# One tanh over the 2304 score columns of a pair of heads

## The chip, the cores and the metric

The kernel runs on one core of a Trainium2 chip. The metric is the device time of one execution in microseconds (us). Five engines work side by side, each through its own list of instructions in order: TensorE (PE, matmuls; PEld is its weight load), VectorE (DVE), ScalarE (ACT), GpSimd (POOL) and SyncE (SP, which issues DMAs). They order their work by semaphores.

## The reference, cut to what matters

The first layer is causal attention with 16 heads of width 8 over 16 batches of 512 rows, with capped scores:

```
scores = jnp.einsum('bhqd,bhkd->bhqk', q, k) / jnp.sqrt(jnp.float32(dk))
scores = jnp.tanh(scores / SOFTCAP) * SOFTCAP
scores = jnp.where(causal[None, None], scores, -jnp.inf)
probs = jax.nn.softmax(scores, axis=-1)
```

It is followed by an output projection, a layer norm, and a second layer that routes 63 rows of each batch through a small attention and an MLP, and another layer norm. `x` is (16, 512, 128) in float32.

## The kernel before, in words

**Groups.** Two heads of a batch are a group; a batch has 8 groups, and the kernel works through 128 of them. The causal scores of a group are kept in transposed blocks: 8 blocks of 64 keys, block kb with 512 - 64 kb query columns, 2304 columns in all, on 128 partitions (64 for each head). They lie in `ps_s`, five PSUM banks; there is only one such buffer. `COL` gives each block's column; the blocks 0, 1 and 7 fill columns 0 to 1023 (two banks), the others columns 1024 to 2303 (three banks).

**The loop.** `iterations` runs `body(p)` for the pairs of batches, each with 16 slots (`for s in range(16)`), and each slot has two halves. Every engine runs the same loop over its own list. PE is one group ahead: in slot s it computes the scores of group s+1 (`scores`, L1186), unit 0 (6 matmuls, 1024 columns) at the start of the first half and unit 1 (10 matmuls, 1280 columns) at the start of the second. Behind each stand the side steps of that half from the table `PE_ORDER`: the preparation of the next batches (`prep.`), probabilities times values (`pv.`, L1202), the end of the first layer (`fin.`), the routing (`route.`), and the second layer of the pairs before (`sel.`, `att.`, `late.`). DVE, POOL and ACT have tables of their own. This order is written out by hand, and each engine keeps to it: a step that waits holds up all behind it.

**ACT.** In slot s ACT computes the tanh of group s in two instructions, one for each unit (L720, `ps_s` to `th`, which has two halves), then a side step if there is one, and then the exp of group s-1 (L735, `th` to the ring `pr`), over all 2304 columns in one instruction. The tanh waits for its unit's scores and for the exp of group s-2.

**Waits of the scores.** A unit of scores waits until the tanh of the same unit of the group before is done (`tanh_done`), as it overwrites what that tanh reads. The other unit can still be read meanwhile.

**Behind the exp.** POOL multiplies the diagonal blocks by a triangle (L631); `pv.0` and `pv.1` need the groups 0 to 3 of a batch, `pv.2` and `pv.3` the groups 4 to 7. SP turns q and k of a later batch by DMA (L549, `turn`) into a buffer whose last reader are the scores of the batch two before.

**Side steps named below.** Of slot 15: `sel.RT` and `prep.xT` (L1225). Slot 0: `sel.msel`, `fin.y0T` | `att.S0`, `prep.qk0`, `att.S1`. Slot 1: `pv.2`, `route.thr` | nothing. Slot 2: `pv.3`, `prep.qk1` | `att.P0`, `prep.v` (L1240). Slot 6: `att.wo` (L1382) | `route.wrow`, `att.h2T` (L1387). Slot 8: `prep.qk0`, `prep.qk1` (L1232) | `fin.y0T` (L1208) and others. Slot 10: `route.won`, `prep.v` (L1240) | `fin.y1T`, `late.w2` (L1400). The bar parts the halves. Slots 4, 7, 9, 11, 12 and 13 have nothing in the first half, so that the two units stand together.

Of the kernel before, what the change touches and what calls it, by code (L numbers as in the profile page):

```python
# [8 lines left out]
ACT = mybir.ActivationFunctionType  # L9
# [7 lines left out]
H, DH = 16, 8  # L17
# [6 lines left out]
SOFTCAP = 50.0  # L24
# [3 lines left out]
QK_SCALE = 64.0  # L28
# [9 lines left out]
NB = S // 64  # L38
COL = {0: 0, 1: 512, 7: 960, 2: 1024, 6: 1408, 3: 1536, 5: 1856, 4: 2048}
GROUP = 2304  # L40
UNIT = ((0, 1024), (1024, GROUP))
UNIT_BLOCKS = ((0, 1, 7), (2, 6, 3, 5, 4))
SIX_FROM = 48
PV_BLOCKS = ((0, 1), (2, 3, 4, 5, 6, 7))

# [1 line left out]
def probs_at(n):  # L47

    return GROUP * (n % 5 if n < SIX_FROM else (5, 3, 4, 0, 1, 2)[(n - SIX_FROM) % 6])


def pv_of(n):

    return 4 * (n // 8) + 2 * (n % 8 // 4) + 2
# [268 lines left out]
def build(nc, x, w_q, w_k, w_v, w_o, amask, pos, router_w, router_b, wq, wk, wv, wo, w1, w2, ln1, ln2, out):  # L323
    ctx = ExitStack()
    with ctx:
        def sb(name, shape, dt=F32):
            return ctx.enter_context(nc.sbuf_tensor(name, shape, dt))

        def sem(name):
            return ctx.enter_context(nc.semaphore(name))  # L330
# [45 lines left out]
        th = sb("th", [P, 2, GROUP])  # L376
# [70 lines left out]
        ps_s = ctx.enter_context(nc.psum_tensor("ps_s", [P, 5 * 512], F32))  # L447
# [17 lines left out]
        scores_ready = sem("scores_ready")  # L465
        tanh_done = sem("tanh_done")
        exp_done = sem("exp_done")
# [22 lines left out]
        def iterations(body):  # L490

            for p in range(-1, PAIRS + 3):
                body(p)

        def run_side(order, table, p, s, half):

            for entry in order[2 * s + half]:
                name, shift = entry.split("@")
                name, _, k = name.partition("/")
                unit = Batch(p + int(shift), int(k)) if k else p + int(shift)  # L500
                if live(unit, B if k else PAIRS):
                    table[name](unit, unit.k if isinstance(unit, Batch) else None)

        def group(p, s, lag=0):

            s -= lag
            b = Batch(p, s // 8)
            return (b, b.k, s % 8) if live(b, B) else None
# [3 lines left out]
        def _(sp):  # L512
# [30 lines left out]
            def turn(b, k):  # L543

                if b.at_least(2):
                    sp.wait_ge(scores_ready, (b - 1).no * 16)
                for s, (dst, part) in enumerate(((q_st, "q"), (k_st, "k"))):
                    pl["prep"].wait(sp, b, f"lo_{part}")
                    sp.dma_start_transpose(out=dst[:, k].rearrange("p g (t n) -> p (g t) n", t=NT),  # L549
                                           in_=st[:, s].rearrange("p g t j c d -> p (g t j c d)")).then_inc(turned[k], 16)  # L550
# [144 lines left out]
        @block.scalar  # L695
        def _(act):
            act.wait_ge(setup_ve, SETUP_RED)
            nc.scalar.activation(turn[:, :, :, :], red[:, :, :, :], ACT.Sin).then_inc(setup_act, 1)

            def att_exp(q, _):  # L700
                ve["att"].wait(act, q, "sub1")
                nc.scalar.activation(pm[:, :, 0:KSEL], pm[:, :, 0:KSEL], ACT.Exp).then_inc(probs_ready, 1)  # L702

            def att_tanh(q, _):
                pl["att"].wait(act, q, "hu")
                nc.scalar.activation(hq[:, :], hu[:, :], ACT.Tanh, scale=float(np.sqrt(2.0 / np.pi)))\  # L706
                    .then_inc(gate_ready, 1)

            table = {"att.exp": att_exp, "att.tanh": att_tanh}

            def body(p):
                for s in range(16):
                    g = group(p, s)
                    if g:
                        b, _, gi = g
                        for u, (c0, c1) in enumerate(UNIT):
                            act.wait_ge(scores_ready, b.no * 16 + (2 * gi + u + 1))
                            if gi >= 2 or b.at_least(1):
                                act.wait_ge(exp_done, b.no * 8 + (gi - 1))
                            nc.scalar.activation(th[:, gi % 2, c0:c1], ps_s[:, c0:c1], ACT.Tanh,  # L720
                                                 scale=1.0 / (QK_SCALE ** 2 * DH ** 0.5 * SOFTCAP))\
                                .then_inc(tanh_done, 1)
                    for half in range(2):
                        run_side(ACT_ORDER, table, p, s, half)
                    g = group(p, s, 1)
                    if g:
                        b, _, gi = g
                        act.wait_ge(tanh_done, b.no * 16 + (2 * gi + 2))

                        n = b.no * 8 + gi  # L730
                        if n >= 5 and n != SIX_FROM:
                            act.wait_ge(pv_done, pv_of(n - (5 if n < SIX_FROM else 6)))
                        if n == SIX_FROM:
                            pe["sel"].wait(act, 1, "R")
                        nc.scalar.activation(pr[:, probs_at(n):probs_at(n) + GROUP], th[:, gi % 2, :], ACT.Exp,  # L735
                                             scale=SOFTCAP).then_inc(exp_done, 1)
            iterations(body)


# [420 lines left out]
        def _(t_):  # L1160
# [15 lines left out]
                tr(ps_y[:, P:P + NPC], pos_f[:, :], ident[0:NPC, 0:NPC])  # L1176
                mm(ps_y[:, 256:257], ones1[:, :], rb_one[:, :], start=True, stop=True).then_inc(setup_pe, 1)

            def scores(b, k, gi, u):

                if gi > 0 or b.at_least(1):
                    t_.wait_ge(tanh_done, b.no * 16 + (2 * gi + u - 1))
                for kb in UNIT_BLOCKS[u]:
                    for s in range(2):
                        rows = slice(32 * (2 * (gi % 2) + s), 32 * (2 * (gi % 2) + s) + 32)
                        last = mm(ps_s[64 * s:64 * s + 64, COL[kb]:COL[kb] + S - 64 * kb],  # L1186
                                  k_st[rows, k, gi // 2, 64 * kb:64 * kb + 64], q_st[rows, k, gi // 2, 64 * kb:S],
                                  start=True, stop=True)
                last.then_inc(scores_ready, 1)
# [234 lines left out]
            def body(p):  # L1424
                for s in range(16):
                    for half in range(2):
                        g = group(p, s, -1)
                        if g and g[2] == 0 and half == 0:
                            t_.wait_ge(turned[g[1]], g[0].pair * 32 + 32)
                        if g:  # L1430
                            scores(g[0], g[1], g[2], half)
                        run_side(PE_ORDER, table, p, s, half)
            iterations(body)


# [26 lines left out]
```

## Time and profile before

| | |
|---|---|
| median of 3 runs | 853.38 us (852.76 to 853.59) |
| profiled execution | 853.79 us, span 851.8 us |
| TensorE clock granted, mean | 0.794 of full speed |
| PE busy | 695.6 us (82%) |
| DVE busy | 588.6 us (69%) |
| ACT busy | 555.5 us (65%) |
| POOL busy | 389.1 us (46%) |

The span runs from the first to the last instruction. Busy is the time in which an engine had an instruction in work; it doesn't say whether anything waited for that work. The view by windows shows the granted clock of a stretch: 1.00 is 2.4 GHz, 0.50 is 1.2 GHz. A row of the timeline gives the start, the duration from first start to last end, the engine, the line, what is written from what is read, the count, and in brackets the idle time before it with what ended it. Ends of matmuls are modelled: the last of a step overlaps the first of the next by some 0.07 us, so that differences of starts are the better measure.

### The profile page before, as it was taken

Reading aid. Unit: us, or ns where it says so; the run is one execution under the profiler, and the core shown is the slowest. Engines: PE = TensorE matmul, PEld = TensorE weight load, DVE = VectorE, ACT = ScalarE, POOL = GpSimd, SP = SyncE. Lnnn points to the kernel's source line nnn. Section 1 sums busy time; section 2 is a strip of 40 time slices with the busy share of each in tenths; the row PEclk is TensorE's granted clock in tenths of the full one; section 3 lists DMA queues with packets and bytes.
Section 4 is the critical chain, followed back from the end, with each engine's and each line's share of the span. In section 5 each row is a group of like instructions: output and inputs, shape, how many; then the busy total and the mean of one; then the engine's idle time right before and its main releaser. Section 6 shows DMA issues by size and latency. Waiting matters only on the chain.

```text
span 851.8 us, 17007 instructions
## 1 busy us (share of the span) xinstructions
PE 695.6 (82%) x6576; PEld 417.3 (49%) x6576; DVE 588.6 (69%) x1681; ACT 555.5 (65%) x403; POOL 389.1 (46%) x399
## 2 busy tenths in 40 slices
PE   3578797998899987898799978998799879874652
PEld 2334344544466454646465545645565545534332
DVE  4442627767768778859676788768785876678355
ACT  0588788879767985877666885868696878600000
POOL 5264435447445663365354654447435644321201
PEclk8567767899769986897697987798798977985755
DMA  6320303033302320030303030220203030000001
GB/s 185 62 52 25 62 13 63 14 65 110 62 14 41 85 53 23 27 75 2 75 27 63 14 63 15 54 47 10 54 27 62 2 62 27 13 1 22 4 0 50
DMA packets 96914, 36.75 MB, mean 43 GB/s; under 512 B 68019, under 2 KB 94147, under 8 KB 96835
## 3 DMA queue, kind: packets, MB, share of 16 engines
q1 hardware_dynamic: 96834, 35.67, 18.4%
q8 instruction: 53, 0.87, 0.4%
q14 instruction: 27, 0.21, 0.1%
HBM read 14.69 MB, written 4.19 MB: 22 GB/s over the span
## 4 chain that ended last, share of the span: by engine, by line
PE 59%; DVE 19%; issue 10%; ACT 8%; POOL 2%; DMA 1%; POOLq 0%; DVEq 0%; ACTq 0%
PE ps_y L1202 16%; PE ps_s L1186 14%; ACT pr L735 4%; ACT th L720 3%; PE ps_a L1232 2%; PE ps_m L1208 2%; PE ps_m L1232 2%; PE ps_m L1356 2%; DVE v_aug L848 2%; PE ps_m L1310 2%; PE ps_m L1260 2%; PE ps_a L1370 2%; PE ps_a L1208 2%; PE ps_a L1393 1%; PE ps_a L1260 1%
## 5 line engine op out<-in xcount | busy, mean ns | idle before, releaser
L720 ACT ACTIVATE th<-ps_s 128x1024 f32<-128x1024 f32 (+1 forms) x256 | 281.1, 1129 | 125.3 <-PE ps_s L1186 116.1
L735 ACT ACTIVATE pr<-th 128x2304 f32<-128x2304 f32 x128 | 271.4, 2121 | 22.2 <-PE ps_y L1202 22.2
L631 POOL TENSOR_TENSOR pr<-pr,tri 128x320 f32<-128x320 f32 (+1 forms) x256 | 193.6, 781 | 182.4 <-ACT pr L735 182.4
L1186 PE MATMUL ps_s<-q_st,k_st 32*64 32x448 f16 (+7 forms) x2048 | 197.7, 332 | 24.8 <-ACT th L720 21.2
L1202 PE MATMUL ps_y<-pr,v_aug 128*32 128x512 f32 (+7 forms) x2048 | 157.2, 451 | 0.4 <-POOL pr L631 0.4
L1186 PEld LDWEIGHTS ps_s<-q_st,k_st 32*64 32x64 f16 x2048 | 95.5, 119 | 116.4 <-issue 44.0
L1202 PEld LDWEIGHTS ps_y<-pr,v_aug 128*32 128x32 f32 x2048 | 61.6, 116 | 76.5 <-issue 58.2
L645 POOL TENSOR_TENSOR st<-qk,st 128x1024 f16<-128x1024 f32 x32 | 73.8, 2326 | 38.9 <-DVE st L864 38.9
L633 POOL TENSOR_TENSOR k_wide<-qkT,head_of 128x1024 f32<-128x1024 f32 x16 | 30.1, 1903 | 65.4 <-DVE qkT L1033 65.4
L633 POOL TENSOR_TENSOR r<-x,rw_row 128x512 f32<-128x512 f32 x16 | 18.9, 1182 | 77.2 <-DVE x L926 77.2
L706 ACT ACTIVATE hq<-hu 128x512 f32<-128x512 f32 x8 | 5.0, 630 | 59.6 <-POOL hu L633 59.6
L874 DVE COPY y_u<-ps_y 128x512 f32<-128x512 f32 x32 | 21.6, 676 | 30.6 <-PE ps_y L1202 30.6
L633 POOL TENSOR_TENSOR st<-qk 128x1024 f32<-128x1024 f32 x16 | 30.9, 1929 | 21.8 <-DVE qk L837 21.7
L950 DVE SCALAR_TENSOR_TENSOR wins<-w_wide,x,later 128x512 f16<-128x512 f32 (+1 forms) x64 | 38.9, 608 | 1.9
L702 ACT ACTIVATE pm<-pm 128x1008 f32<-128x1008 f32 x8 | 8.3, 1037 | 42.7 <-DVE pm L1047 42.7
L633 POOL TENSOR_TENSOR z_base<-x,coef 128x512 f32<-128x512 f32 x16 | 17.1, 1070 | 39.5 <-DVE coef L974 39.5
L1310 PE MATMUL ps_m<-mask_a,E 128*64 128x512 f32 x112 | 29.8, 610 | 0.0
L848 DVE COPY v_aug<-ps_m 64x512 f32<-64x512 f32 x32 | 22.0, 689 | 9.8 <-PE ps_m L1240 9.3
L1232 PE MATMUL ps_m<-wT,xT 128*128 128x256 f32 x64 | 26.5, 556 | 0.9 <-DVE xT L832 0.9
L1387 PE MATMUL ps_m<-ident,hn 128*128 128x128 f32 x8 | 3.4, 430 | 28.2 <-DVE hn L1086 28.2
L1232 PE MATMUL ps_a<-wT,xT 128*128 128x256 f32 x64 | 25.0, 530 | 0.1
L1356 PE MATMUL ps_m<-k_wide,qkT 128*64 128x512 f32 x64 | 19.9, 701 | 4.5 <-POOL k_wide L633 2.7
(223 smaller groups left out, 1136.8 us busy)
## 6 DMA issues: line engine op xcount, KB each, us to landing
x_in<-in_L_attn_x SPq DMA_DIRECT2D x16, 256.0 KB, 2.8
x_res<-in_L_attn_x SPq DMA_DIRECT2D x16, 256.0 KB, 3.1
result<-y_out SPq DMA_DIRECT2D x16, 256.0 KB, 2.4
mask_a<-in_L_ffn_attention_mask SPq DMA_DIRECT2D x3, 1024.0 KB, 5.5
pr<-in_L_ffn_attention_mask SPq DMA_DIRECT2D x2, 1024.0 KB, 8.6
w_sb<-in_L_ffn_w SPq DMA_DIRECT2D x2, 256.0 KB
q_st<-st SPq DMA_TRANSPOSE x16, 4.5
k_st<-st SPq DMA_TRANSPOSE x16, 4.8
```

What stands on the lines that cost most here:

```text
L631: return nc.gpsimd.tensor_tensor(buf, buf, tri[:, None, :].to_broadcast([P, blocks, 64]), ALU.mult)
L633: mul = lambda out, a, b: nc.gpsimd.tensor_tensor(out, a, b, ALU.mult)
L645: pl["prep"].done(nc.gpsimd.tensor_tensor(lo_parts[s], qk_twice[s], hi_parts[s], ALU.subtract), f"lo_{part}", b)
L720: nc.scalar.activation(th[:, gi % 2, c0:c1], ps_s[:, c0:c1], ACT.Tanh, scale=1.0 / (QK_SCALE ** 2 * DH ** 0.5 * SOFTCAP))\
L735: nc.scalar.activation(pr[:, probs_at(n):probs_at(n) + GROUP], th[:, gi % 2, :], ACT.Exp, scale=SOFTCAP).then_inc(exp_done, 1)
L848: ve["prep"].done(nc.vector.tensor_copy(v_aug[rows, k].rearrange("p b n c -> p (b n) c")[:, :, 16 * s:16 * s + DH], at("prep.v", b)[rows, ...
L950: step(lambda: nc.vector.scalar_tensor_tensor(won[c], w_wide[:, P * c:], x1[:, k, c, D:D + 1], later[:, 0:n], ALU.is_le, ALU.mult, accum_o ...
L1186: last = mm(ps_s[64 * s:64 * s + 64, COL[kb]:COL[kb] + S - 64 * kb], k_st[rows, k, gi // 2, 64 * kb:64 * kb + 64], q_st[rows, k, gi // 2, ...
L1202: last = mm(ps_y[32 * j:32 * j + 32, 64 * kb:S], v_aug[:, k, kb, gi, :], pr[:, c:c + S - 64 * kb], start=(kb == 0), stop=(kb == NB - 1), s ...
L1232: last = mm(at(f"prep.qk{i}", b)[:, :].rearrange("p (n t e) -> p n t e", t=2, e=32)[:, :, t % 2], xT[:, P * t:P * t + P], wT[:, 0:2, :].re ...
L1310: last = mm(at("sel.R")[SLOTS * k:SLOTS * k + SLOTS, :], E[:, c, SLOTS * k:SLOTS * k + SLOTS], (mask_b if k and q < 2 else mask_a)[:, c, : ...
L1356: last = mm(at(f"att.S{h}")[rows, :], qkT[:, 0, rows], k_wide[:, k, 8 * h:8 * h + 8, :].rearrange("p h s -> p (h s)"), start=True, stop=True)
```

## The change

The two units become one: PE computes all 16 matmuls of a group at the start of the slot's first half, after the tanh of the whole group before; ACT computes one tanh over 2304 columns, when all of the group's scores are there. The semaphores count 8 steps a batch instead of 16. SP's wait for the scores of a whole batch is the same event in the new count. The side steps keep their halves and their order.

```diff
-UNIT = ((0, 1024), (1024, GROUP))
-UNIT_BLOCKS = ((0, 1, 7), (2, 6, 3, 5, 4))
+BLOCKS = (0, 1, 7, 2, 6, 3, 5, 4)
@@ turn (SP)
-                    sp.wait_ge(scores_ready, (b - 1).no * 16)
+                    sp.wait_ge(scores_ready, (b - 1).no * 8)
@@ body (ACT)
-                        for u, (c0, c1) in enumerate(UNIT):
-                            act.wait_ge(scores_ready, b.no * 16 + (2 * gi + u + 1))
-                            if gi >= 2 or b.at_least(1):
-                                act.wait_ge(exp_done, b.no * 8 + (gi - 1))
-                            nc.scalar.activation(th[:, gi % 2, c0:c1], ps_s[:, c0:c1], ACT.Tanh,
-                                                 scale=1.0 / (QK_SCALE ** 2 * DH ** 0.5 * SOFTCAP))\
-                                .then_inc(tanh_done, 1)
+                        act.wait_ge(scores_ready, b.no * 8 + (gi + 1))
+                        if gi >= 2 or b.at_least(1):
+                            act.wait_ge(exp_done, b.no * 8 + (gi - 1))
+                        nc.scalar.activation(th[:, gi % 2, :], ps_s[:, 0:GROUP], ACT.Tanh,
+                                             scale=1.0 / (QK_SCALE ** 2 * DH ** 0.5 * SOFTCAP)).then_inc(tanh_done, 1)
...
-                        act.wait_ge(tanh_done, b.no * 16 + (2 * gi + 2))
+                        act.wait_ge(tanh_done, b.no * 8 + (gi + 1))
@@ scores, body (PE)
-            def scores(b, k, gi, u):
+            def scores(b, k, gi):
                 if gi > 0 or b.at_least(1):
-                    t_.wait_ge(tanh_done, b.no * 16 + (2 * gi + u - 1))
-                for kb in UNIT_BLOCKS[u]:
+                    t_.wait_ge(tanh_done, b.no * 8 + gi)
+                for kb in BLOCKS:
...
-                        if g:
-                            scores(g[0], g[1], g[2], half)
+                        if g and half == 0:
+                            scores(g[0], g[1], g[2])
```

## Rows read from the trace of the kernel before

**Rows 1.** Page, part 1: busy us, share of the span, instructions.
```profile
PE 695.6 (82%) x6576; PEld 417.3 (49%) x6576; DVE 588.6 (69%) x1681; ACT 555.5 (65%) x403; POOL 389.1 (46%) x399
```

**Rows 2.** Page, part 4: chain that ended last, share by engine.
```profile
PE 59%; DVE 19%; issue 10%; ACT 8%; POOL 2%; DMA 1%; POOLq 0%; DVEq 0%; ACTq 0%
```

**Rows 3.** Groups of ACT by form: count, busy us, mean ns, idle before.
```profile
L735 ACT ACTIVATE pr<-th 128x2304 f32<-128x2304 f32 x128 | 271.4, 2121 | 22.2 <-PE ps_y L1202 22.2
L720 ACT ACTIVATE th<-ps_s 128x1280 f32<-128x1280 f32 x128 | 158.0, 1234 | 60.9 <-PE ps_s L1186 60.1
L720 ACT ACTIVATE th<-ps_s 128x1024 f32<-128x1024 f32 x128 | 131.1, 1024 | 64.4 <-PE ps_s L1186 56.0
```

**Rows 4.** Waits: us in total, times, longest.
```profile
ACT th L720 <- PE ps_s L1186: 116.1, 66, 3.9
...
PE ps_s L1186 <- ACT th L720: 21.2, 26, 2.8
```

**Rows 5.** Timeline of PE: score blocks of 6, 10 and 16 matmuls, and followers.
```profile
597.80 0.62 PE L1186 MATMUL ps_s<-q_st,k_st 32*64 32x512 f16 x6
598.35 0.49 PE L1382 MATMUL ps_a<-wo,oT 128*128 128x128 f32 x2
...
614.89 0.73 PE L1186 MATMUL ps_s<-q_st,k_st 32*64 32x384 f16 x10
...
618.79 1.17 PE L1186 MATMUL ps_s<-q_st,k_st 32*64 32x512 f16 x16
619.89 2.48 PE L1202 MATMUL ps_y<-pr,v_aug 128*32 128x384 f32 x48
```

**Rows 6.** Timeline of PE and of ACT, slots 15 and 0.
```profile
562.63 0.62 PE L1186 MATMUL ps_s<-q_st,k_st 32*64 32x512 f16 x6
...
565.03 0.62 PE L1186 MATMUL ps_s<-q_st,k_st 32*64 32x512 f16 x6
...
563.29 1.02 ACT L720 ACTIVATE th<-ps_s 128x1024 f32<-128x1024 f32 x1 [1.25 <-PE ps_s L1186]
```

**Rows 7.** Timeline of PE, slots 1 and 2.
```profile
570.80 0.62 PE L1186 MATMUL ps_s<-q_st,k_st 32*64 32x512 f16 x6
...
573.35 0.82 PE L1186 MATMUL ps_s<-q_st,k_st 32*64 32x384 f16 x16
574.10 2.48 PE L1202 MATMUL ps_y<-pr,v_aug 128*32 128x384 f32 x48
576.50 1.13 PE L1232 MATMUL ps_m<-wT,xT 128*128 128x256 f32 x4
...
579.01 1.15 PE L1240 MATMUL ps_m<-wT,xT 128*64 128x64 f32 x32
```

**Rows 8.** Timeline of PE, slot 6, second half.
```profile
603.84 0.36 PE L1387 MATMUL ps_m<-ident,hn 128*128 128x128 f32 x1 [3.76 <-DVE hn L1086]
```

**Rows 9.** Timeline of PE, slot 8.
```profile
610.76 1.06 PE L1186 MATMUL ps_s<-q_st,k_st 32*64 32x512 f16 x6
611.75 2.08 PE L1232 MATMUL ps_m<-wT,xT 128*128 128x256 f32 x4
...
615.79 0.63 PE L1208 MATMUL ps_a<-ident,y_u 128*128 128x128 f32 x4 [0.17 <-issue]
```

**Rows 10.** Timeline of ACT and of PE, slot 10.
```profile
621.77 2.15 ACT L720 ACTIVATE th<-ps_s 128x1024 f32<-128x1024 f32 x2
...
622.85 0.62 PE L1186 MATMUL ps_s<-q_st,k_st 32*64 32x512 f16 x6 [0.48 <-ACT th L720]
...
623.76 1.15 PE L1240 MATMUL ps_m<-wT,xT 128*64 128x64 f32 x32
...
626.95 1.13 PE L1400 MATMUL ps_m<-w_sb,hu 128*128 128x128 f32 x8 [0.79 <-DVE v_aug L848]
```

**Rows 11.** Windows: length, busy us of each engine (count), PE clock, DMA.
```profile
604.00:614.20 10.20, 8.84 (x52) 6.28 (x52) 8.92 (x32) 5.30 (x4) 5.02 (x6) 0.50 0.01 2
```

## The prediction, made before the changed kernel ran

> **What bounds the kernel now.** I read the page's busy times first, then the chain of waits, then the waits, and last the timeline of one pair of batches, slot by slot, with PE and ACT beside each other. The busy times show PE at 82% of the span and ACT at 65% [rows 1]. The chain gives PE 59%, DVE 19%, ACT 8% [rows 2]. So the end is set by PE's list, with pieces where PE waits for a short run of DVE steps, and ACT is on it only in places. The waits say the same from ACT's side: ACT stood 116.1 us for scores, PE only 21.2 us for a tanh [rows 4]. The timeline shows that PE nearly always has its next step ready; so what the change does to ACT's busy time matters little, and what it does to the moment at which PE may go on matters everywhere.
>
> **ACT's part.** Two tanh of 1.024 and 1.234 us go, one comes [rows 3]. From the two, a column costs (1234 - 1024) / 256 = 0.82 ns, so 2304 columns cost 1234 + 1024 x 0.82 = 2074 ns. Bounds: the exp over as many columns took 2121 ns [rows 3], the sum of the two 2258. I take 2.07. The gain is not 2258 - 2074: a pair that runs back to back took 2.15 us from start to end [rows 10], as the two overlap. It is 0.08 us a group, and only where ACT is on the chain. ACT holds 8% of it, about half of that tanh, some 25 pairs of pieces: about -2 us in all.
>
> The Trainium skill, "ScalarE: Activation LUTs", section "What ACT_TABLE_LOAD costs", gives an ACTIVATE 186 ns and 0.833 ns a column, and lets neighbours overlap by about 93 ns. By it the new tanh takes 2105 ns, an estimate from that page, and each merge saves 93 ns. The trace agrees within a few per cent. By the page alone, with ACT as the bound, 128 merges would give back 12 us; that is the end of the faster rival below, whose working from rows stands there.
>
> **PE's part, what it saves.** A block of 6 score matmuls takes PE 0.55 us (598.35 - 597.80), the block of 10 takes 0.73 - 0.07 = 0.66, and 16 in one run 1.10 (619.89 - 618.79) [rows 5]. So where a slot has side steps between the units, joining them saves 0.11 us. Slots 14 and 0 are such places: -0.11 each. In slots 4, 7, 9, 11, 12 and 13 the units stand together already: nothing. In slot 3 both units fall into waits for DVE before and after: nothing. Slot 5 runs at the lower clock and gains or loses about nothing.
>
> **PE's part, what it adds.** PE gets `ps_s` back only after the whole tanh. From the start of a block of 16, its scores are there after 1.17 us [rows 5], ACT starts 0.04 later (562.63 + 0.62 to 563.29 [rows 6]), runs 2.07, and PE starts 0.06 behind its end (621.77 + 1.02 to 622.85 [rows 10]). That is 3.34 us at least from one block's start to the next. Whatever is queued behind the waiting block on PE, that is all side steps of the slot, waits with it. A slot whose side steps are long hides this. I go through those that don't, in the pair that starts at 565.03.
>
> - Slots 15 to 0: the blocks start 2.40 us apart (562.63, 565.03 [rows 6]), now 3.34. +0.94.
> - Slots 1 and 2: the side steps of slot 1 take 573.35 - 570.80 - 0.55 = 2.00, so PE is ready at 3.10 and waits 0.24 more. `pv.3` starts 4.44 behind slot 1's start, not 3.30: +1.14 [rows 7]. Here unit 1 of slot 1 and unit 0 of slot 2 had stood together and taken 0.75 for 16 matmuls, since neighbouring groups use other rows of the array; that is lost. Unit 1 of slot 2 no longer stands behind `prep.qk1` (-0.66), but `prep.v` at 579.01 needs DVE's copy of what qk1 wrote. Bounds +0.48 and +1.14. I take +0.55, as DVE had been held by another step and has some slack.
> - Slot 6: `att.wo` follows the block, and DVE's long run behind it ends in the 3.76 us wait before h2T [rows 8]. The block ahead of wo grows from 0.55 to 1.10; unit 1 was behind wo, in time that PE spends waiting anyway. +0.55.
> - Slot 8: the same with qk0 and qk1 ahead of y0T, which waits for DVE's copy; unit 1 had filled that wait. The stretch runs at clock 0.50 [rows 11], where 6 matmuls took 0.99 (611.75 - 610.76 [rows 9]) and 16 take double of 1.10. Bounds +0.55 and +1.2, by when the clock comes back. I take +0.8.
> - Slot 10: ACT is late here, since its side tanh waits for POOL. Tanh of the group starts at 621.77, so PE goes on at 621.77 + 2.07 + 0.06 = 623.90 and not at 622.85: +1.05. The block ahead of `prep.v` is 0.55 longer: +1.60 there; w2 waits for DVE's copy of v [rows 10]. Lower bound +0.94 (the unit behind v is gone). I take +1.25.
>
> Sum of a pair: 0.94 - 0.11 - 0.11 + 0.55 + 0.55 + 0.8 + 1.25 = 3.87 us. All of these lie on PE's list or on DVE runs that PE waits for, so they add up.
>
> **The kernel's sum.** Four of the eight pairs have all stages, and the same rows recur in them: 4 x 3.87 = 15.5. The first three have fewer side steps and in parts ACT as the bound; there a group costs ACT 2.12 + 2.15 before and 2.12 + 2.07 after, so the delays partly vanish. The last has no preparation in slots 8 and 10. I take half the rate for these four, 7.8, bounds 0 and 15.5. With ACT's -2: +21.3. From the profiled execution's 853.79 this gives 875.1; that execution lay 0.4 above the median of the runs, so 874.7, told as 875. Behind the last scores (736 us on) there is no change.
>
> What costs nothing: the SP wait is the same event. The exp and the masks behind it come earlier by up to the time that unit 1 stood behind side steps; PE hardly ever waits for them, so it is worth nothing, as POOL's and ACT's slack hides it.
>
> **The rivals.**
> A. The clock turns it worse. In 604.00 to 614.20 PE ran at 0.50, and it had stood 3.76 us just before [rows 8, 11]. The change adds some 20 us of waiting in PE's list. If that brings one third more of such a stretch in each pair, 3.4 us at half clock that cost 1.7 each, it is 8 x 1.7 = +14: 889 us. For it: the added waits lie close to those that were there. Against: joined blocks make dense work. The Trainium skill, "TensorE: Matmul & The Clock Gate", section "A second HAM failure mode: psum-queue depth-cycling", says that short pauses between groups of matmuls suffice to swing the clock down and up. The trace agrees in that its clock swings many times in one pair.
>
> B. The delays are absorbed. If the waits for DVE have more slack than I give them, only slots 15 to 0 and 10 cost, (0.94 + 0.94 - 0.22) x 4 = 6.6, less ACT's 2: 858. Near that lies no change.
>
> C. Faster. The mechanism is ACT's lead: with all scores issued early in the slot, ACT never stands for unit 1 [rows 4], tanh and exp run ahead, and PE finds `ps_s` free each time. Then only the savings remain: ten slots of a pair join two blocks, slots 1 and 2 lose their run of 16, so nine times 0.11, in eight pairs -8, and ACT's -2: 844. It decides from the point at which a slot's side steps take over 2.2 us behind the block (3.34 - 1.10). Slots 15 and 1 have less (1.3 and 2.0 us), and slot 10 is late on ACT for another reason, which speaks against it.
>
> D. The whole tanh is dearer than I think, 2.26 as the two together: 0.19 more at three places in eight pairs, +4. It widens the forecast's own range.
>
> **How the numbers follow.** Forecast with D: 0.62, own range 864 to 884. A: 0.13. B: 0.12, a third of it within the bound of no change. C: 0.13. What a measurement here can tell from no change is 0.2%, 1.7 us. Slower 0.62 + 0.13 + 0.08 = 0.83, same 0.04, faster 0.13. The range 855 to 889 leaves out C, the low end of B and the top of A.
>
> **What would show it.** After: ACT rows at L720 x128 near 2074 ns; ACT's wait for scores well below 116 us; PE's waits for a tanh up from 21.2 to 40 or more, at slots 0, 2 and 10; block starts in slots 15 to 0 3.34 us apart; the L1186 blocks all of 16 and 1.10 us at full clock; full pairs some 4 us longer. Wrong would be: these waits stay near 21 us (C), or they grow and the pairs don't (B), or the mean clock falls by more than 0.02 with PE busy up (A).

## The result, and the profile after

The changed kernel takes 902.94 us (median of 4 runs, 902.01 to 908.19), the kernel before 853.07 in the same comparison (850.15 to 853.59): 1.0601 times the time, 95% interval 1.0559 to 1.0643. The forecast was slower by 22 us; it came out slower by 50, outside the range. The profiled execution took 908.19 us with a span of 906.2 and a mean clock of 0.768 (before: 853.79, 851.8, 0.794). Medians and ranges here and below are of all executions; the ratios leave out those that lie more than 1.5% above the fastest of their kernel (two of e2, one each of e8 and e10, three of e15).

The page of after, busy times and chain of waits; they answer to [rows 1, 2]:

```profile
PE 711.7 (79%) x6576; PEld 439.3 (48%) x6576; DVE 595.3 (66%) x1681; ACT 542.6 (60%) x275; POOL 385.4 (43%) x399
...
PE 57%; DVE 14%; ACT 13%; issue 11%; POOL 3%; DMA 1%; POOLq 0%; SPq 0%; DVEq 0%; ACTq 0%
```

The first line splits the loss in two. Span less PE's busy time is the time in which PE stood: 851.8 - 695.6 = 156.2 before, 906.2 - 711.7 = 194.5 after, +38.3. PE's busy time grew by 711.7 - 695.6 = 16.1, with the same 6576 matmuls. 38.3 + 16.1 = 54.4, the whole difference of the spans. ACT's share of the chain rose from 8% to 13%.

The 16.1 are a difference of two things. The sums over all windows with a granted clock of 0.50, before and then after:

```profile
sum 350.25, PE 272.23 PEld 164.03 DVE 246.12 ACT 187.43 POOL 151.00; mean PE 9.72 PEld 5.86 DVE 8.79 ACT 6.69 POOL 5.39
```

```profile
sum 420.15, PE 322.80 PEld 205.14 DVE 279.80 ACT 200.77 POOL 151.69; mean PE 10.76 PEld 6.84 DVE 9.33 ACT 6.69 POOL 5.06
```

PE did 322.8 - 272.2 = 50.6 us more of its work at the low clock. What that costs can be taken from two kernels below with the same 6592 matmuls, e11 and e14: 302.5 against 254.3 us at the low clock, 709.9 against 687.7 us busy, so 22.2 / 48.2 = 0.46 us for each. By this the clock cost some 23 us, an estimate, and the joined blocks gave back some 7. The prediction's working for rival C had 8 for that saving.

Groups of ACT by form in after [rows 3], and its waits [rows 4]:

```profile
L732 ACT ACTIVATE pr<-th 128x2304 f32<-128x2304 f32 x128 | 270.8, 2116 | 42.6 <-PE ps_y L1199 42.6
L718 ACT ACTIVATE th<-ps_s 128x2304 f32<-128x2304 f32 x128 | 267.7, 2092 | 154.6 <-PE ps_s L1183 149.4
```

```profile
ACT th L718 <- PE ps_s L1183: 149.4, 78, 6.3
...
PE ps_s L1183 <- ACT th L718: 49.7, 43, 4.6
```

The whole tanh takes 2.09 us, as priced. PE's wait for a tanh went from 21.2 to 49.7 us, and ACT's wait for scores from 116.1 to 149.4: each engine now stands while the other works.

Timeline of PE in after, the slots of a full pair (start, duration); they answer to [rows 5 to 10]:

```profile
606.18 1.17 PE L1183 MATMUL ps_s<-q_st,k_st 32*64 32x512 f16 x16
...
609.53 1.17 PE L1183 MATMUL ps_s<-q_st,k_st 32*64 32x512 f16 x16 [1.16 <-ACT th L718]
...
615.19 1.17 PE L1183 MATMUL ps_s<-q_st,k_st 32*64 32x512 f16 x16
...
618.55 1.17 PE L1183 MATMUL ps_s<-q_st,k_st 32*64 32x512 f16 x16 [0.19 <-ACT th L718]
619.65 2.48 PE L1199 MATMUL ps_y<-pr,v_aug 128*32 128x384 f32 x48
...
623.97 1.15 PE L1237 MATMUL ps_m<-wT,xT 128*64 128x64 f32 x32 [0.34 <-DVE qk L834]
...
645.85 1.17 PE L1183 MATMUL ps_s<-q_st,k_st 32*64 32x512 f16 x16
...
652.26 0.48 PE L1384 MATMUL ps_m<-ident,hn 128*128 128x128 f32 x1 [3.77 <-DVE hn L1083]
...
659.19 2.13 PE L1183 MATMUL ps_s<-q_st,k_st 32*64 32x512 f16 x16
...
665.19 0.63 PE L1205 MATMUL ps_a<-ident,y_u 128*128 128x128 f32 x4 [0.83 <-issue]
...
673.32 1.17 PE L1183 MATMUL ps_s<-q_st,k_st 32*64 32x512 f16 x16 [1.55 <-ACT th L718]
...
677.92 1.13 PE L1397 MATMUL ps_m<-w_sb,hu 128*128 128x128 f32 x8 [1.40 <-DVE v_aug L845]
```

The terms can be taken from one row to the next: slots 15 to 0 609.53 - 606.18 = 3.35 (2.40 before); slot 1 to `pv.3` 619.65 - 615.19 = 4.46; slot 6's block to h2T 652.26 - 645.85 = 6.41 (6.04); slot 8's block to y0T 6.00 (5.03, 610.76 to 615.79); slot 10's block to w2 is in the fifth point of the reasons below.

### The profile page after: what moved, and what is told of

It is laid out like the page before. It is cut to its first block, busy times and chain, and to the rows that moved or that the text cites. A ratio compares the mean times of both kernels' runs of the same rounds, so it can differ in the third digit from the quotient of the medians.

```text
span 906.2 us, 16753 instructions
## 1 busy us (share of the span) xinstructions
PE 711.7 (79%) x6576; PEld 439.3 (48%) x6576; DVE 595.3 (66%) x1681; ACT 542.6 (60%) x275; POOL 385.4 (43%) x399
## 4 chain that ended last, share of the span: by engine, by line
PE 57%; DVE 14%; ACT 13%; issue 11%; POOL 3%; DMA 1%; POOLq 0%; SPq 0%; DVEq 0%; ACTq 0%
PE ps_s L1183 16%; PE ps_y L1199 13%; ACT th L718 8%; ACT pr L732 5%; PE ps_a L1367 3%; PE ps_m L1229 2%; PE ps_a L1229 2%; PE ps_m L1205 2%; PE ps_m L1353 2%; DVE v_aug L845 2%; PE ps_a L1292 2%; PE ps_m L1307 2%; PE ps_a L1205 1%; PE ps_m L1237 1%; PE ps_a L1390 1%
## 5 line engine op out<-in xcount | busy, mean ns | idle before, releaser
L718 ACT ACTIVATE th<-ps_s 128x2304 f32<-128x2304 f32 x128 | 267.7, 2092 | 154.6 <-PE ps_s L1183 149.4
L732 ACT ACTIVATE pr<-th 128x2304 f32<-128x2304 f32 x128 | 270.8, 2116 | 42.6 <-PE ps_y L1199 42.6
L630 POOL TENSOR_TENSOR pr<-pr,tri 128x320 f32<-128x320 f32 (+1 forms) x256 | 189.8, 767 | 195.0 <-ACT pr L732 194.8
L1183 PE MATMUL ps_s<-q_st,k_st 32*64 32x512 f16 (+7 forms) x2048 | 192.3, 338 | 53.3 <-ACT th L718 49.7
L1183 PEld LDWEIGHTS ps_s<-q_st,k_st 32*64 32x64 f16 x2048 | 101.5, 124 | 134.5 <-ACT th L718 47.4
L947 DVE SCALAR_TENSOR_TENSOR wins<-w_wide,x,later 128x512 f16<-128x512 f32 (+1 forms) x64 | 37.0, 579 | 1.9
L845 DVE COPY v_aug<-ps_m 64x512 f32<-64x512 f32 x32 | 22.0, 688 | 11.1 <-PE ps_m L1237 10.5
L1367 PEld LDWEIGHTS ps_a<-vv,k_wide 128*128 128x128 f32 x128 | 27.2, 322 | 1.2 <-DVE k_wide L1056 1.2
L1367 PE MATMUL ps_a<-vv,k_wide 128*128 128x32 f32 x128 | 27.0, 386 | 0.9 <-DVE k_wide L1056 0.9
L834 DVE COPY qk<-ps_m 128x512 f32<-128x512 f32 x16 | 11.1, 691 | 23.4 <-PE ps_m L1229 23.4
```

The lines of the kernel that those rows point to most:

```text
L630: return nc.gpsimd.tensor_tensor(buf, buf, tri[:, None, :].to_broadcast([P, blocks, 64]), ALU.mult)
L718: nc.scalar.activation(th[:, gi % 2, :], ps_s[:, 0:GROUP], ACT.Tanh, scale=1.0 / (QK_SCALE ** 2 * DH ** 0.5 * SOFTCAP)).then_inc(tanh_done, 1)
L845: ve["prep"].done(nc.vector.tensor_copy(v_aug[rows, k].rearrange("p b n c -> p (b n) c")[:, :, 16 * s:16 * s + DH], at("prep.v", b)[rows, ...
L947: step(lambda: nc.vector.scalar_tensor_tensor(won[c], w_wide[:, P * c:], x1[:, k, c, D:D + 1], later[:, 0:n], ALU.is_le, ALU.mult, accum_o ...
L1367: last = mm(at("att.PV")[:, 32 * n:32 * n + 32], PT[:, n, :], vv[:, n, :, :].rearrange("p k c -> p (k c)"), start=True, stop=True)
```

## Experiments

In most of them two functions decide for each of the 128 groups, by its number n: `joined(n)` puts unit 1 right behind unit 0 in the first half, and `one_tanh(n)` makes one tanh of the two. Both true for all n is the changed kernel. The edit all of them share:

```diff
-                        for u, (c0, c1) in enumerate(UNIT):
+                        whole = one_tanh(b.no * 8 + gi)
+                        for u, (c0, c1) in enumerate(((0, GROUP),) if whole else UNIT):
...
-                            scores(g[0], g[1], g[2], half)
+                            late = not joined(g[0].no * 8 + g[2])
+                            if half == 0 or late:
+                                scores(g[0], g[1], g[2], half)
+                            if half == 0 and not late:
+                                scores(g[0], g[1], g[2], 1)
```

### The two halves of the change, and a buffer freed early

e1: scores joined, two tanh.

```diff
+def joined(n): return True
+def one_tanh(n): return False
```

> All 16 score matmuls of a group at the start of the slot, but still two tanh pieces, each of which frees its own banks. Theory W (PE waits for the whole tanh before it may overwrite the scores, and the pauses also lower its clock): the second piece of 10 matmuls must still wait for the end of the second tanh, only the first 6 may go 1 us earlier, so most of the loss stays: 880 to 900 us. Rival O (the order alone costs: 10 matmuls moved ahead of the side steps of the first half): the whole loss stays, 900 to 905 us. Rival T (the long tanh as such): 853 us.

890.53 us (888.61 to 894.21), ratio 1.0442, interval 1.0405 to 1.0479, inside the 880 to 900 expected. PE's standing time grew by 22.5 us, its busy time by 13.9. More than half of the loss comes without the merged tanh.

e2: scores at their old places, one tanh.

```diff
+def joined(n): return False
+def one_tanh(n): return True
```

> One tanh over 2304 columns, with the scores still in two pieces at their old places in the slot. Theory W: the tanh can only start after the second piece, and only the side steps of the second half hide it, so PE waits more than in the changed kernel: 920 us or more, and PE's waits for a tanh over 60 us (49.7 in the changed kernel, 21.2 before). Rival O: no loss, 850 to 856 us, as the order on PE is that of before.

908.54 us (897.43 to 914.9), 1.0568 [1.0496, 1.064]; the ratio is of the executions at 897.43 and 906.09, the second of which is profiled. Waits of PE and ACT in e2:

```profile
ACT th L730 <- PE ps_s L1196: 191.0, 96, 6.3
...
PE ps_s L1196 <- ACT th L730: 72.6, 52, 3.9
```

One tanh alone costs as much as the whole change (standing time +41.1); joining on top of it adds nothing. The two parts aren't additive: one tanh puts block and tanh in series, wherever the second unit stands. That it would be dearer than the changed kernel was right in direction for PE's wait (72.6 against 49.7), but not in the time, where 920 and more was expected and the intervals overlap.

e3: joined, but `ps_s` is freed after 1024 columns. The tanh of the other 1280 columns reads a constant in SBUF, so the scores of those columns are left out of the result.

```diff
+                            nc.scalar.activation(th[:, gi % 2, 0:1024], ps_s[:, 0:1024], ACT.Tanh,
...
+                                .then_inc(tanh_done, 2)
+                            nc.scalar.activation(th[:, gi % 2, 1024:GROUP], later[:, 0:1].to_broadcast([P, GROUP - 1024]), ACT.Tanh,
+                                                 scale=0.02).then_inc(filled, 1)
```

> The changed kernel's order on PE, but the tanh that frees the scores covers only 1024 columns (1.02 us); a second one of 1280 columns over a constant follows, so that ACT's load is that of before. This leaves out the tanh of the columns from 1024 on. Theory W: the block starts of slots 15 and 0 come within 2.4 us again, PE's waits for a tanh fall below 15 us, and the time falls to 855 to 868 us; what stays over 853 is the order's own cost (slots 6 and 8, some 1.4 us in each of 7 pairs). Rival O: 895 us or more.

883.78 us (880.5 to 886.13), 1.0351 [1.0308, 1.0394]. The expectation failed. Its wait:

```profile
PE ps_s L1201 <- ACT th L732: 29.2, 22, 3.6
```

Freeing the buffer a microsecond early takes back 49.7 - 29.2 = 20.5 us of that wait, but of PE's standing time only 38.3 - 23.7 = 14.6. What is left, 23.7, is near e1's 22.5. Of these, 8.0 are still waits for a tanh (29.2 against 21.2; in e1, with 28.2, they are 7.0); the rest, some 16 in both, is the order, side steps behind a whole block.

### Where it is lost: late and early pairs

e4 makes the change for the pairs 3 to 7 only, e5 for the pairs 0 to 2 only.

```diff
+# e4, both functions
+    return n >= 48
+# e5, both functions
+    return n < 48
```

> The change in the groups from 48 on alone (the last five of eight pairs); the first three pairs as before. In the profile of the changed kernel the first three pairs are 29 us longer than before and the rest 25. If the loss arises where the waits are, in each pair by itself, this run gives 853 + 25 = 878 us (872 to 884). My prediction's own rates (3.9 us for a full pair) give 867. If the loss of the first pairs is only a shift of the phase of the clock that later pairs inherit, it gives over 890.

883.14 us (878.78 to 883.18), 1.0338 [1.0302, 1.0373], inside the 872 to 884 expected.

> The change in the groups below 48 alone (the first three of eight pairs), the counterpart of the run with the last five. If the loss arises pair by pair, the first three keep their 20 to 29 us and the rest is as before: 875 to 882 us, and the two halves add up to the whole (30 + 25 against 50). My prediction's rate for these pairs gives 859. If the later pairs inherit a worse phase of the clock, it is over 888.

897.96 us (893.09 to 903.93), 1.0502 [1.0451, 1.0553]. The busy times of e4 (span 881.2) and of e5 (span 902.1):

```profile
PE 710.6 (81%) x6576; PEld 434.5 (49%) x6576; DVE 598.6 (68%) x1681; ACT 546.8 (62%) x323; POOL 387.5 (44%) x399
```

```profile
PE 722.1 (80%) x6576; PEld 442.0 (49%) x6576; DVE 588.0 (65%) x1681; ACT 551.7 (61%) x355; POOL 386.2 (43%) x399
```

Standing time: e4 170.6 (+14.4), e5 180.0 (+23.8). Together 38.2, and the changed kernel has 38.3: this part adds up. (To a tenth only by luck: e6, e11 and e14 below, in which hardly a wait is edited, stand 2.7 to 3.2 us longer than the kernel before.) Busy time: +15.0 and +26.5, together 41.5, where the changed kernel has 16.1: this part does not add up. So there are two causes, and the second isn't a price for each edited slot.

The second is plain in the pairs 3 to 7 of e5, which run the code of before. Windows of three such pairs in e5, and of the same pairs before (length, busy of PE, PEld, DVE, ACT, POOL, clock, DMA):

```profile
415.20:514.30 99.10, 89.13 (x822) 56.52 (x821) 72.60 (x208) 69.29 (x51) 46.95 (x47) 0.78 0.19 39
514.30:610.20 95.90, 85.97 (x822) 52.44 (x821) 71.19 (x208) 69.07 (x51) 47.41 (x47) 0.80 0.18 40
610.20:705.80 95.60, 85.75 (x822) 52.43 (x821) 71.18 (x208) 69.08 (x51) 47.39 (x47) 0.80 0.18 37
```

```profile
377.10:472.70 95.60, 85.58 (x822) 52.48 (x821) 70.89 (x208) 69.10 (x51) 47.53 (x47) 0.80 0.18 40
472.70:565.00 92.30, 82.58 (x822) 50.47 (x821) 71.24 (x208) 69.11 (x51) 47.44 (x47) 0.85 0.19 41
565.00:657.20 92.20, 82.59 (x822) 50.48 (x821) 71.27 (x208) 69.13 (x51) 47.47 (x47) 0.85 0.18 38
```

Each has 822 matmuls, and length less PE's busy time is nearly the same (9.97, 9.93, 9.85 against 10.02, 9.72, 9.61): no new wait. Only clock and busy time differ. e5 expected 888 and more for this case.

### Single slots

e6 joins only the groups of slots 14 and 15, from n = 47 on, with two tanh; e7 joins the groups that slots 6 and 8 issue, in all pairs, with two tanh; e8 gives both parts of the change to the groups that slots 15 and 9 issue, whose tanh are the ones of slots 0 and 10.

```diff
+# e6, joined; one_tanh is False
+    return n >= 47 and n % 16 in (15, 0)
+# e7, joined; one_tanh is False
+    return n % 16 in (7, 9)
+# e8, joined and one_tanh
+    return n % 16 in (0, 10)
```

> The kernel before, with two tanh pieces; only in slots 14 and 15 from the end of the third pair on, the second piece of scores follows the first at once. There its banks have long been read, and the trace of the run with all blocks joined shows 0.27 us saved in each such slot. Theory: 5 pairs x 0.54 = 2.7 us saved, 850.5 us. Rival, the phase of the clock: a start moved by half a microsecond lets a stretch at the low clock come or go, and the time moves by 2 us or more either way.

861.28 us (859.73 to 868.49), 1.0107 [1.0068, 1.0147]; in the profiled execution, the longest of the six, standing +2.7, busy +12.2. The expected 2.7 us didn't come. The timeline has the savings (slot 14 takes 571.44 - 566.86 = 4.58 us, before 558.68 - 553.83 = 4.85), but PE's work at the low clock grew from 272.2 to 303.1 us, which costs several times as much.

> The kernel before, with two tanh pieces; only the score blocks of slots 6 and 8 joined, so that 10 matmuls stand ahead of the side steps that DVE's runs wait for. No tanh is longer and no wait for a tanh should grow. My terms: 0.55 + 0.8 a pair, in 6 to 7 pairs +8 to +9: 862 us. Rival (the order costs more, since the added pauses lower the clock): +12 to +20, 865 to 873 us. If joining is free: 853.

861.45 us (10 runs, 854.23 to 864.7), 1.0082 [1.0049, 1.0115]; standing +10.8, where the two terms gave 8 to 9. The runs lie at two levels, five at 854 to 859 and five at 864 to 865; the profiled one (858.52) has 5.9 us less busy time than before.

> The kernel before, except the groups 0 and 10 of each pair, which have one tanh over 2304 columns and one block of scores, so that PE waits for a whole tanh at the start of slots 0 and 10 alone. My terms: 0.94 + 1.05 a pair, less 0.2 for the joined block: +1.8 in eight pairs, 867 us. Rival (the waits lower the clock as well): half-clock time grows by 20 us or more over that of before and the time passes 872. Absorbed: 853 to 858.

884.36 us (872.31 to 885.89), 1.0314 [1.025, 1.0379]. The profiled run, 872.31, stood 11.9 us more; the rest of its loss, 6.7, is PE's busy time. The other three runs lie 12 us higher, and what they spent it on isn't in a profile.

### The clock by itself

If PE's pauses make the clock fall, filling one should raise it. e9 puts three matmuls of 512 columns into the wait ahead of h2T [rows 8] in the kernel before; e10 does the same in the changed kernel. They write the bank that the transpose behind them overwrites.

```diff
-                ve["att"].wait(t_, q, "hn2")
                 bank_free("att.h2T", q)
+                for _ in range(3):
+                    mm(at("att.h2T")[:, :], ident[:, :], later[:, :], start=True, stop=True)
+                ve["att"].wait(t_, q, "hn2")
```

> The kernel before, with 3 float32 matmuls of 512 columns (some 3 us of PE work, result overwritten) in slot 6 where PE stands 3.76 us for DVE; behind that pause the clock is at 0.50 for 10.2 us in each full pair. Theory C (the pauses on PE's list cost a second time through the clock): the stretch behind slot 6 runs at full clock, half-clock time falls by 50 us or more, PE's busy time without the added 21 us falls, and the time falls to 820 to 845 us. Rival: PE's pauses are not what lowers the clock, or the filler comes in the way: 853 to 865 us.

856.01 us (12 runs, 850.98 to 862.91), 1.0046 [1.0016, 1.0076]: the expectation failed. The mean clock rose from 0.794 to 0.823 (0.817 to 0.832 over the 12 executions, against 0.792 to 0.801 before), and PE's busy time by 12.6 us, with 25.4 us of filler in it (six times 2.74, 4.70 and 4.21), so that the other matmuls took some 13 less. Nothing of it reached the end. Timeline of PE in e9, slots 6 to 8:

```profile
605.41 2.74 PE L1387 MATMUL ps_m<-later,ident 128*128 128x512 f32 x6
...
609.32 0.33 PE L1389 MATMUL ps_m<-ident,hn 128*128 128x128 f32 x1 [1.17 <-DVE hn L1086]
609.58 1.17 PE L1186 MATMUL ps_s<-q_st,k_st 32*64 32x512 f16 x16
...
611.90 0.83 PE L1225 MATMUL ps_m<-ident,x_in 128*128 128x128 f32 x4 [1.15 <-issue]
...
615.89 0.16 PE L1273 MATMUL ps_a<-count,ident 128*128 128x4 f16 x1 [1.46 <-issue]
```

The block of 16 behind h2T takes 1.17 us here, not the 2.13 of half clock. Then PE stands 1.15 us, and 1.46 two steps on. The first of them waits for a copy by DVE (`h2T`, L1089), which starts 611.45 - 609.32 = 2.13 us behind h2T here and 605.96 - 603.84 = 2.12 in the kernel before: DVE is as late as it was, and a faster PE waited longer.

> The changed kernel with the same filler in slot 6. Theory C: it gains too, by 10 to 35 us from 903, to 868 to 893; and the difference between this run and the filled kernel before is then nearer to the 38 us that the waits alone account for than the 50 us of today. Rival: no gain, 900 to 910.

902.87 us (900.88 to 914.71), 1.0571 [1.054, 1.0602]: no gain over the changed kernel either, though the clock rose here too: 0.808 to 0.812 in the three executions that the ratio counts, 0.768 to 0.780 in the changed kernel. The profiled execution of e10 is the one at 914.71, so its trace isn't read here.

The next runs leave the tanh and the scores alone and add work to the kernel before: `sel.msel`, 16 matmuls and 0.9 us in one slot 0, is issued twice, once in the whole kernel. From first start to last end it then takes 1.54 us in e11 and e14 and not 0.97, so that the work added is some 0.6 us long. e11 does it in the fourth pair, e15 only with half of the matmuls, e14 in the sixth pair, e13 in the changed kernel; e12 adds four transposes in the setup, where PE idles.

```diff
-                for k in range(2):
+                for k in (0, 1, 0, 1) if q == 1 else (0, 1):   # e11, e13; e14: q == 3
+                for k in (0, 0, 1) if q == 1 else (0, 1):      # e15
```

> The kernel before with 16 matmuls (0.9 us of PE work) repeated once, in slot 0 of the fourth pair; all other pairs untouched. If a delay only costs its own length, 854 us. If later pairs inherit another phase of the clock, as the pairs 3 to 7 seem to have done in the run with the change in the early groups alone (same code, same waits, 20 us longer), the time moves by 4 us or more, 857 to 875.

872.12 us (870.7 to 873.44), 1.0218 [1.0192, 1.0244]. 0.6 us of work costs 18.8 (853.36 before in this comparison). The busy times of e11 (span 869.3) and the pair that follows the added step:

```profile
PE 709.9 (82%) x6592; PEld 432.9 (50%) x6592; DVE 592.1 (68%) x1681; ACT 555.9 (64%) x403; POOL 387.6 (45%) x399
...
481.50:577.40 95.90, 85.97 (x824) 52.43 (x823) 71.19 (x208) 69.13 (x51) 47.42 (x47) 0.80 0.18 40
```

Standing +3.2, busy +14.3 of which 0.6 is the step. The pair is the 95.9 us one of e5 again, to a hundredth in its busy time (85.97), though the two edits have nothing in common; the code of this pair is that of before in both.

> The kernel before with four transposes more in the setup, in the 12 us in which PE stands at the start. They delay nothing. If the rhythm depends only on when the later work falls against itself, 853 us. If anything that moves the start against the clock's own rhythm ends it, 858 to 875.

854.52 us (10 runs, 851.37 to 856.14), 1.0015 [0.9991, 1.0039]: no change. Four instructions more, in a place where nothing waits for PE, cost nothing.

> The changed kernel with the 0.9 us step in slot 0 of the fourth pair that cost the kernel before 19 us. If the changed kernel is already out of the favourable rhythm, it costs its own length: 902 to 906 us, and the change costs only 30 to 34 us between the two kernels with the step. If the step costs 19 us here too, 920.

908.5 us (906.05 to 911.06), 1.0657 [1.0609, 1.0705]. In the changed kernel the same step costs 5.6. With the step in both, the two kernels are 908.5 - 872.1 = 36.4 us apart; their profiles, 39.6 apart, differ by 34.6 in standing time (194.0 against 159.4) and by 5.0 in PE's busy time (714.9 against 709.9).

> The kernel before with the 0.9 us step in the sixth pair instead of the fourth. If the pairs behind the step inherit the worse rhythm (some 3.4 us each), two pairs fewer pay: 858 to 865 us. If the loss isn't tied to the pairs behind, 872.

849.54 us (10 runs, 848.05 to 851.48), 0.9962 [0.9941, 0.9982]: with more work, faster than the kernel before by 3.9 (853.39 in this comparison). Windows of the pair ahead of the added step and of the one with it:

```profile
378.90:467.10 88.20, 77.68 (x822) 47.55 (x821) 71.44 (x208) 68.97 (x51) 47.76 (x47) 0.90 0.22 43
467.10:560.00 92.90, 83.24 (x841) 51.11 (x839) 70.78 (x208) 69.18 (x51) 47.60 (x47) 0.85 0.19 41
```

The first row is code that the edit doesn't touch, and it ran ahead of the edit: 88.2 us at a clock of 0.90, where before took 95.6 at 0.80. The step can't have brought that about, and e12, which has no step, shows the same. Its windows of the same pair and the next:

```profile
381.20:469.40 88.20, 77.67 (x823) 47.58 (x821) 71.43 (x208) 68.97 (x51) 47.73 (x47) 0.90 0.22 43
469.40:564.00 94.60, 84.87 (x823) 53.13 (x821) 73.58 (x208) 69.18 (x51) 48.04 (x47) 0.82 0.20 40
```

So e14, which up to there executes the instructions of the kernel before, takes 7 us less for a single pair. What can be the step's doing is the stretch from the sixth pair on, 92.9 us against e12's 94.6. How it does it is open. In e11, too, a part of the difference lies ahead of its step: its second pair took 80.1 us, before 83.5. e14 is the one version that beats both kernels, by PE's busy time alone (-7.9, standing +2.9); I don't call it an improvement of the kernel.

> The kernel before with half the step (8 matmuls, 0.45 us) in the fourth pair. If the rhythm tips at a point, the loss is all or nothing: 853 to 855 or 868 to 873 us. If it is in proportion, 862.

Four executions: 855.5, 871.35, 872.15, 871.57. One lies 2 us above the kernel before, three some 18, near the whole step's 18.8, and none at half. The one at 855.5 is profiled, so what the other three spent isn't in a profile, and four executions are too few to call the response a step; that stays a reading.

## Why the prediction was wrong

1. **What bounds the kernel** was read rightly. PE's list sets the end, and delaying PE costs though ACT gets less to do (busy 555.5 to 542.6).

2. **The tanh**: predicted 2.07 us, measured 2.092. Right. The 2 us credited to ACT's overlap don't show anywhere; ACT stood longer by more than that. They were also counted too high: the page of before gives the tanh 3% of the chain and not half of ACT's 8%, which is some 12 groups and 1.0 us.

3. **The series of block and tanh**: predicted 3.34 us from block to block, measured 3.35 at full clock. Right there, and e2 shows it is enough by itself. The side remark that ACT's wait for scores would fall well below 116 us was wrong (149.4): I looked at unit 1, which no longer comes late, and forgot that the only tanh now waits for the whole block (e1, with the block joined and two tanh, has 109.9).

4. **Slots 1 and 2, 6 and 8**: predicted +0.55, +0.55, +0.8. `pv.3` stood 4.46 behind slot 1's start (predicted 4.44), and v 623.97 - 615.19 = 8.78 behind, before 579.01 - 570.80 = 8.21, so +0.57. Slot 6 +0.37, slot 8 +0.97. e7, with these two alone, has 10.8 us more standing time, against 8 to 9 at the rate of my terms in the six to seven pairs that have these steps.

5. **Slot 10**: predicted +1.25; in after w2 starts 677.92 - 671.18 = 6.74 behind the start of ACT's tanh, before 626.95 - 621.77 = 5.18 [rows 10]: +1.56, near the upper bound of 1.60, since nothing absorbed the added 0.55 of the block. The terms of a full pair, with -0.27 and -0.11 in slots 14 and 0, come to 4.04 for 3.87. The pair itself grew by 8.9 (101.1 against 92.2): slots 3 to 5 took 20.80 us (625.05 to 645.85) for 17.71 (580.09 to 597.80), at a clock of 0.67 for 0.81, and in slot 12 PE stood 1.9 us longer, mostly for DVE's `xs`, a wait that I had no term for.

6. **The kernel's sum, first failed step.** "there a group costs ACT 2.12 + 2.15 before and 2.12 + 2.07 after, so the delays partly vanish", and "I take half the rate for these four". For the late pairs the sum was of the right size, if somewhat high: 15.5 and the last pair's 1.9 predicted, 17.4, and +14.4 of standing time in e4, some 10 with what its joined blocks save in busy time (PE worked 313.4 us at the low clock, 41.2 more than before; 15.0 - 0.46 x 41.2 is -4). For the three early pairs I had 5.8, and e5 shows +23.8, some 21 on the same count (336.4 us at the low clock). Windows of the first pair, before and then after:

```profile
33.90:110.20 76.30, 61.77 (x559) 32.44 (x558) 31.95 (x60) 65.07 (x48) 34.93 (x36) 0.68 0.21 43
```

```profile
35.60:122.40 86.80, 62.34 (x556) 33.57 (x557) 30.39 (x59) 64.01 (x32) 34.66 (x36) 0.66 0.18 37
```

It is 10.5 us longer, while both engines do the same work: PE 61.77 and 62.34 us, ACT 65.07 and 64.01. Five blocks of that pair on PE, and ACT between the third and the fourth, in after:

```profile
51.04 2.12 PE L1183 MATMUL ps_s<-q_st,k_st 32*64 32x512 f16 x16
55.35 2.12 PE L1183 MATMUL ps_s<-q_st,k_st 32*64 32x512 f16 x16 [2.19 <-ACT th L718]
...
67.95 1.17 PE L1183 MATMUL ps_s<-q_st,k_st 32*64 32x512 f16 x16
72.60 1.73 PE L1183 MATMUL ps_s<-q_st,k_st 32*64 32x512 f16 x16 [3.49 <-ACT th L718]
...
76.70 2.13 PE L1183 MATMUL ps_s<-q_st,k_st 32*64 32x512 f16 x16 [1.33 <-ACT th L718]
```

```profile
61.84 2.09 ACT L718 ACTIVATE th<-ps_s 128x2304 f32<-128x2304 f32 x1 [0.21 <-PE ps_s L1183]
68.15 2.12 ACT L732 ACTIVATE pr<-th 128x2304 f32<-128x2304 f32 x1 [4.22 <-PE ps_y L1199]
70.37 2.09 ACT L718 ACTIVATE th<-ps_s 128x2304 f32<-128x2304 f32 x1
```

The same place before:

```profile
46.56 2.12 PE L1186 MATMUL ps_s<-q_st,k_st 32*64 32x512 f16 x16
49.19 2.40 PE L1186 MATMUL ps_s<-q_st,k_st 32*64 32x512 f16 x16 [0.50 <-ACT th L720]
...
58.77 2.48 PE L1202 MATMUL ps_y<-pr,v_aug 128*32 128x384 f32 x48
61.17 1.17 PE L1186 MATMUL ps_s<-q_st,k_st 32*64 32x512 f16 x16
64.75 2.31 PE L1186 MATMUL ps_s<-q_st,k_st 32*64 32x512 f16 x16 [2.41 <-ACT th L720]
```

```profile
61.37 2.12 ACT L735 ACTIVATE pr<-th 128x2304 f32<-128x2304 f32 x1 [1.26 <-PE ps_y L1202]
```

Two things add up here. The first is the series of block and tanh at the low clock, where the block takes 2.12 us and not 1.17: 55.35 - 51.04 = 4.31 from block to block, before 49.19 - 46.56 = 2.63, +1.68. I had priced the series at full clock alone.

The second is in the other blocks. An exp needs room in the ring `pr`, which a `pv.` step frees. ACT stood 4.22 us for it in after and 1.26 before; in the whole kernel 42.6 us, against 22.2 [rows 3]. The next tanh stands behind that exp, and PE's next block now waits for all of that tanh: 72.60 - 67.95 = 4.65 from block to block, before 64.75 - 61.17 = 3.58, +1.07. That is slot 10's term, which I had priced at +1.05 and counted once a pair, in the full pairs; in the first pair alone PE stands more than 1 us longer in five slots (1 and 3 are of the first kind, 6 is the one shown, and 10 and 14). An engine at its bound had been read as cover. But there, as I read these rows, ACT is at its bound only in stretches, with `pv.` steps between in which PE is, and each change from one to the other costs the part of the tanh that no longer overlaps.

7. **The clock, second failed step and the larger one.** The forecast had no term for it: 875 is added up at the clock of before, and 0.13 stood on rival A, "the mean clock falls by more than 0.02 with PE busy up". It fell by 0.026 with PE's busy time up by 16.1; on the count above the clock cost some 23 us, where A had 14. What brings it down is shown in part. Filling one wait raises it (e9, e10), so PE's waits have a share in it, as A had it; but no time came back with it. That the added waits account for the 23 us isn't shown: e6 stands 2.7 us more and is busy for 12.2 more, e11 3.2 and 14.3, and e7 stands 10.8 us more and is busy for 5.9 less. The Trainium skill, "TensorE: Matmul & The Clock Gate", section "A second HAM failure mode: psum-queue depth-cycling", describes a clock that swings because of short pauses between groups of matmuls. The runs agree that the clock swings in a kernel of this kind and rises when a pause is filled; no run here gives a price for each pause added.

8. **The rivals.** B (absorbed) and C (faster) are out: every term showed, and e3 with its buffer free after 1.02 us was still slower by 3.5%. D's dearer tanh is out by the rows.

So: of the profiled execution's 54.4 us, 38.3 are added standing time (14.4 with the change in the late pairs and 23.8 in the early ones, by e4 and e5 apart), some 23 are clock, and the joined blocks give back some 7. The forecast had +21.3 of it. Of the 33.1 above that, some 23 are the clock and some 10 the rest: the early pairs +15, the late ones -7, and ACT's 2. The clock's part and the split are estimates, and the two parts aren't independent, as a slower PE has less left to wait for (e9 shows it the other way round). Against the medians, 50 us apart, the waits' 36 to 38 leave 12 to 14 for PE's busy time. What stays open is what decides which lengths the clock gives a kernel's pairs; the runs show that it does, not by what rule.

## What to carry to other kernels

A buffer that exists once and is filled and drained in two pieces is a pipeline of depth two. Before merging the pieces, take the new time from block to block (fill, drain, both handovers; here 3.35 us at full clock, 4.31 at the low one) and hold it against each slot, in every phase of the kernel: where the drain engine is late the whole drain lies bare, at its bound or not. And split a slower run into standing time (span less busy) and busy time first: the waits that the edit adds are in the former, while the latter mixes what the edit saves with what the clock takes, and moves by 14 us for edits that hardly touch a wait (e11).

## What the runs showed of the hardware

In these kernels the time of PE's work moves, with its clock, by far more than the small shifts of work that were made. The same code, a full pair, took 99.1, 95.9, 95.6, 92.2 or 88.2 us at mean clocks of 0.78, 0.80, 0.80, 0.85 and 0.90; two kernels whose edits have nothing in common (e5, e11) show the pairs of 99.1, 95.9 and 95.6 in the same order. The 88.2 came in two kernels (e12, e14) ahead of any difference in their loops. 16 matmuls added once moved the kernel by +18.8 us in the fourth pair and by -3.9 in the sixth; with 8 of them one execution lay 2 us up and three 18. The same kernel before was a fairly favourable case of this: of the eleven profiled variants of its order (e1 to e8, e11, e14, e15) eight had more busy time on PE, by 6.7 to 26.5 us. For a change expected to bring less than 2% in such a kernel, the time alone does not say whether the idea is good. The standing time says more: e6, e11, e12, e14 and e15, which hardly edit a wait, moved it by 0.8 to 3.2 us, and PE's busy time by -7.9 to +14.3.
